# Five steps of the feed-forward generator, instead of four, per step of the output projection

## The chip, the cores and the metric

The kernel runs on the 8 cores of one Trainium2 chip. Each core computes 2 of 16 batch rows and exchanges nothing with the others. The metric is the device time of the slowest core in microseconds (us).

## The reference

Per batch row x is [2048, 1024]. The kernel computes `x + attention(xn) + ffn(xn)` with `xn` the layer norm of x. The feed-forward part is a loop of three rounds that carries `out`:

```python
out = x                                   # here x is xn
for _ in range(3):
    h = gelu(out @ w1 + b1); h = gelu(h @ w2 + b2); h = gelu(h @ w3 + b3)
    tf = sigmoid(h @ w4 + b4)             # one number per token
    combined = 0.7 * gf + 0.3 * tf        # gf: one number per batch row
    coupling = 0.1 + adaptive_range * (combined - 0.5) * 2.0
    out = out + coupling * twist(out)     # twist: quarters of the columns swapped, two negated
```

The widths are 1024, 1024, 512, 256, 1. The attention part ends with `out @ wo.T`, the output projection.

## The kernel before, in words

`build_program` lets Python generators record operations, and `Prog.emit` appends each to the list of its engine. Every engine runs its own list in the order of recording. `Prog.finalize` adds semaphore waits for true dependencies. All instructions are issued from `Prog.replay`, so the profile gives line 170 for all of them; they are told apart by tile names.

For each of the two batch rows (`for s in range(BATCH)`) come the layer norm (`gen_ln`), eight head pairs of attention (`gen_attention` beside `gen_projembed`), the normalisation (`gen_norm` beside `gen_gc`), and then four quarters of 512 tokens (`for q in range(NQ)`). A quarter has four token tiles of 128 rows, tq = 0 to 3. Only the quarters change. In them stand:

- `gen_ffn(q)`, 58 steps (a step ends at a `yield`). Steps 1 to 4: load an x tile into `xt0` or `xt1` by a DMA on SP, and write the normalised tile into `stream` (DVE). Then three rounds of 18 steps each. Steps 5 to 12, 23 to 30, 41 to 48: w1, a column block each (8 matmuls of 128x512 and a Gelu on ACT); in rounds 2 and 3 the first of them also casts and transposes the four stream tiles (`sbf`, `ofm`). Steps 13 to 16, 31 to 34, 49 to 52: w2. Steps 17 and 18, 35 and 36, 53 and 54: w3. Step 19 (37, 55): w4, tanh, `cpt`, four tiny matmuls, `cptm` and `ncptm`, and the update of stream tile 0 on DVE; the three steps behind it (20 to 22, 38 to 40, 56 to 58): the updates of tiles 1 to 3. An update is one copy into `t01` and four scalar_tensor_tensor.
- `gen_wo(q)`, 12 steps, three per token tile: (a) load the x tile into `xt0` (even tile) or `xt1` (odd tile), and 8 matmuls of `attn_in` by `woTt` into the first half of `ps_s0` or `ps_s1`; (b) 8 matmuls into the second half; (c) `tensor_add` of `ps_s` into the `xt` tile on DVE, and a DMA on SP that stores it into the DRAM scratch `ffn_s`, with the key `partD0` for even tiles and `partD1` for odd ones. The text calls these steps wo 1 to wo 12.
- `gen_final(q)`, recorded when both are done, four times: load a tile from `ffn_s` back into `xt0` or `xt1`, add it to `stream` (DVE), store the sum to `out`.

`drive((gen_ffn(q), 4), (gen_wo(q), 1))` sets the order: four steps of the first, one of the second, and so on until both end. With the rate 4, wo step n is recorded behind ffn step 4n, so wo 12 behind step 48.

The load of `gen_final` names both `partD0` and `partD1` as read:

```python
dma("sync", xb_t[:], ffn_s[s, tb * 128:(tb + 1) * 128, :],
    reads=["partD0", "partD1"], writes=[xb])
```

Of the kernel before, what the change touches and what calls it, by code (L numbers as in the profile page):

```python
# [185 lines left out]
def build_program(S=2048, BATCH=2, DM=1024, NH=16, dbg=False):  # L186
# [196 lines left out]
    def dma(queue, dst, src, reads, writes, note="", no_waw=False, **kw):  # L383
        return E(queue, "dma_start", dst, src, reads=reads, writes=writes, dma=True,
                 no_waw=no_waw, note=note, **kw)
# [116 lines left out]
    def drive(*pairs):  # L502
        gens = [g for g, n in pairs]
        rates = [n for g, n in pairs]
        done = [False] * len(gens)
        while not all(done):
            for gi in range(len(gens)):
                for _ in range(rates[gi]):
                    if not done[gi]:
                        done[gi] = next(gens[gi], _SENT) is _SENT  # L510
    _SENT = object()

    for s in range(BATCH):
# [352 lines left out]
        def gen_wo(q):  # L866
            for tq in range(QTB):
                tb = q * QTB + tq
                pp = tb % 2
                xb = f"xt{tb % 2}"  # L870
                xb_t = xt[tb % 2]
                dma("sync", xb_t[:], x_d[s, tb * 128:(tb + 1) * 128, :], reads=["dx"], writes=[xb])
                for half in range(DM // 512):
                    for c in range(CK):
                        E("tensor", "matmul", ps_s[pp][:, half * 512:(half + 1) * 512],
                          attn_in[c][:, tb * 128:(tb + 1) * 128],
                          woTt[c][:, half * 512:(half + 1) * 512],
                          start=(c == 0), stop=(c == CK - 1),
                          reads=[f"attnin{c}", f"woTtp{c}"], writes=[KS[pp]])
                    yield  # L880
                E("vector", "tensor_add", xb_t[:], ps_s[pp][:, 0:DM], xb_t[:],
                  reads=[KS[pp], xb], writes=[xb])
                dma("sync", ffn_s[s, tb * 128:(tb + 1) * 128, :], xb_t[:],
                    reads=[xb], writes=[f"partD{tb % 2}"], no_waw=True)
                yield
# [125 lines left out]
        def gen_final(q):  # L1011
            for tq in range(QTB):
                tb = q * QTB + tq
                xb = f"xt{tq % 2}"
                xb_t = xt[tq % 2]
                dma("sync", xb_t[:], ffn_s[s, tb * 128:(tb + 1) * 128, :],
                    reads=["partD0", "partD1"], writes=[xb])
                E("vector", "tensor_add", T["stream"][:, tq * DM:(tq + 1) * DM],
                  T["stream"][:, tq * DM:(tq + 1) * DM], xb_t[:],
                  reads=[f"stream{tq}", xb], writes=[f"stream{tq}"])  # L1020
                dma("sync", out_d[s, tb * 128:(tb + 1) * 128, :],
                    T["stream"][:, tq * DM:(tq + 1) * DM],
                    reads=[f"stream{tq}"], writes=[f"outD{tq}"], no_waw=True)
                yield

        for q in range(NQ):
            drive((gen_ffn(q), 4), (gen_wo(q), 1))
            for _ in gen_final(q):
                pass

# [12 lines left out]
def _get_nc(S, BATCH):  # L1043
    key = (S, BATCH)
    if key not in _NC_CACHE:
        _NC_CACHE[key] = build_program(S=S, BATCH=BATCH)
    return _NC_CACHE[key]
# [34 lines left out]
```

How the kernel before makes its waits and increments, by code:

```python
            def _run(engine):  # L164
                for op in self.ops[eng_name]:
                    for (sem, val) in op.waits:
                        engine.wait_ge(sem, val)
                    if op.method is None:
                        continue
                    inst = getattr(engine, op.method)(*op.args, **op.kwargs)
                    if op.inc_pos is not None:
                        kind, tgt = op.inc_pos
                        if kind == "D":
                            inst.then_inc(self.dma_slots[tgt], 16)
                        else:
                            inst.then_inc(self.eng_sems[tgt], 1)
```

## Time and profile before

| | us |
|---|---|
| two runs | 4245.42 and 4086.72, median 4166.07 |
| profiled execution | 4085.43 |
| its span, slowest core (2) | 4083.9 |
| spans of the 8 cores | 4058.0 to 4083.9 |
| PE busy | 2626.8 (64%) |
| DVE busy | 1402.4 (34%) |
| ACT busy | 1642.5 (40%) |

The profile is of core 2. Times in rows are microseconds from the start of the span, and a row of the timeline merges instructions of one kind that follow each other. PE is TensorE, DVE is VectorE, ACT is ScalarE, SPq is the queue of SyncE, which only issues DMAs here. The quarters of the first batch row lie between about 1437 and 2107 us, those of the second between about 3391 and 4084 us.

### The profile page before, as it was taken

The page shows a single profiled execution, that of the slowest core. Times are in us where ns is not written, and L with a number is a line of the kernel's source. Part 1 is how long each engine was busy: PE and PEld are TensorE (multiplying, and loading weights), DVE is VectorE, ACT ScalarE, POOL GpSimd, SP SyncE. Part 2 cuts the span into 40 slices and gives each one's busy share as a digit, 9 for nine tenths or more (in the row PEclk, how much of TensorE's full clock was granted, in tenths as well). Part 3 has the DMA queues.
Part 4 walks back from the last instruction along what each step waited for, and adds up shares of the span by engine and source line. Part 5 has one row for each costly group of instructions (what it writes and reads, how often), then busy time and mean ns, then how long its engine had stood idle before and what let it go on. Part 6 is the DMA issues. An engine that isn't in the chain of part 4 may idle for free.

```text
span 4083.9 us, 35532 instructions; the slowest of 8 cores (4058.0 to 4083.9 us)
## 1 busy us (share of the span) xinstructions
PE 2626.8 (64%) x10297; PEld 1084.6 (27%) x10486; DVE 1402.4 (34%) x2359; ACT 1642.5 (40%) x2082; POOL 40.5 (1%) x80
## 2 busy tenths in 40 slices
PE   0437777677767967567523576777767787666664
PEld 0213222232222223223212222232223212322322
DVE  5353233322332323333346333323332242333333
ACT  2206565566655022122123465666656701222221
POOL 1000000000000000000000000000000000000000
PEclk9959898898888578778666788998889857877776
DMA  6540011100100131121233011001110003022121
GB/s 158 129 82 22 13 27 26 25 8 21 26 19 5 27 91 67 48 92 42 72 110 110 23 26 26 16 11 26 26 25 15 7 13 78 31 93 73 42 83 57
DMA packets 84371, 193.23 MB, mean 47 GB/s; under 512 B 25559, under 2 KB 28632, under 8 KB 84184
## 3 DMA queue, kind: packets, MB, share of 16 engines
q1 hardware_dynamic: 73240, 175.74, 14.4%
q0 software_dynamic: 10944, 15.21, 2.8%
q8 instruction: 91, 1.49, 0.2%
q14 instruction: 96, 0.79, 0.1%
HBM read 134.27 MB, written 41.94 MB: 43 GB/s over the span
## 4 chain that ended last, share of the span: by engine, by line
PE 46%; DVE 22%; DMA 13%; issue 12%; ACT 5%; SPq 1%; DVEq 1%; POOL 0%; ACTq 0%; POOLq 0%
PE ps_w L170 24%; PE ps_s L170 14%; PE ps_pv L170 8%; DVE stream L170 6%; DMA xt<-x 4%; ACT pt L170 3%; DMA tmp<-qmag 3%; DMA xt<-ffn_s 3%; DVE vp L170 2%; DVE qh L170 2%; DVE ke L170 1%; DMA ke<-kmag 1%; SPq L170 1%; DMA w1t<-cnw 1%; DVE tmp L170 1%
## 5 line engine op out<-in xcount | busy, mean ns | idle before, releaser
L170 ACT ACTIVATE pt<-ps_s,cpool 128x1024 bf16<-128x1024 f32 x1024 | 1084.4, 1112 | 818.3 <-PE ps_s L170 814.9
L170 PE MATMUL ps_pv<-pt,vp 128*65 128x512 bf16 x2048 | 662.8, 407 | 291.9 <-DVE tmpB L170 229.6
L170 PE MATMUL ps_s<-qh,ke 128*128 128x512 bf16 x1976 | 645.7, 408 | 114.1 <-ACT pt L170 82.0
L170 PEld LDWEIGHTS ps_pv<-pt,vp 128*65 128x65 bf16 x2048 | 236.5, 118 | 573.6 <-issue 383.8
L170 PEld LDWEIGHTS ps_s<-qh,ke 128*128 128x128 bf16 x2048 | 173.6, 103 | 471.8 <-issue 394.5
L170 ACT ACTIVATE h<-ps_w,b1f 128x512 bf16<-128x512 f32 x192 | 131.9, 687 | 354.0 <-PE ps_w L170 354.0
L170 PE MATMUL ps_w<-ofm,w1t 128*128 128x512 bf16 x994 | 244.9, 405 | 15.5 <-DVE ofm L170 10.4
L170 ACT CAST ofm<-ps_w 128x128 bf16<-128x128 f32 x256 | 49.6, 280 | 457.3 <-PE ps_w L170 457.2
L170 PE MATMUL ps_w<-ident,sbf 128*128 128x128 bf16 x512 | 64.7, 306 | 248.0 <-DVE sbf L170 248.0
L170 DVE COPY rowstg<-ps_pv 1x1024 f32<-1x1024 f32 x32 | 39.1, 1222 | 455.7 <-PE ps_pv L170 455.4
L170 PE MATMUL ps_w<-xnfm,wvt 128*128 128x512 bf16 x498 | 170.2, 476 | 13.1 <-DVE ke L170 8.4
L170 DVE CAST vp<-ps_w 128x64 bf16<-128x64 f32 x512 | 115.6, 226 | 182.0 <-PE ps_w L170 154.3
L170 PE MATMUL ps_w<-ident,tmpv 128*128 128x128 bf16 x256 | 57.1, 223 | 178.2 <-DVE vp L170 170.7
L170 PE MATMUL ps_w<-h,w2t 128*128 128x512 bf16 x750 | 170.0, 379 | 0.9
L170 DVE CAST tmpv<-ps_w 128x512 bf16<-128x512 f32 x64 | 44.2, 691 | 335.3 <-PE ps_w L170 335.3
L170 PE MATMUL ps_s<-woTtp,attnin 128*128 128x512 bf16 x502 | 147.7, 444 | 7.9 <-DMA woTtp<-woT_s 5.1
L170 PE MATMUL ps_w<-xnfm,wqt 128*128 128x512 bf16 x494 | 135.5, 399 | 24.7 <-DMA wqt<-wqT_s 21.4
L170 DVE COPY xsq<-ps_pv 1x1024 f32<-1x1024 f32 x32 | 39.1, 1222 | 322.4 <-PE ps_pv L170 322.4
L170 PE MATMUL ps_w<-ident,xnb 128*128 128x128 bf16 x256 | 33.0, 306 | 175.9 <-DVE xnb L170 169.9
L170 PEld LDWEIGHTS ps_w<-ofm,w1t 128*128 128x128 bf16 x1024 | 104.7, 103 | 149.4 <-issue 46.0
L170 PE MATMUL ps_s<-rcps,onesf 1*64 1x512 f32 x128 | 116.8, 1063 | 36.3 <-DMA rcps<-rowsums 36.3
L170 PE MATMUL ps_w<-xnfm,wkt 128*128 128x512 bf16 x499 | 130.0, 384 | 6.1 <-DVE ke L170 2.8
(128 smaller groups left out, 2608.9 us busy)
## 6 DMA issues: line engine op xcount, KB each, us to landing
xt<-x SPq DMA_DIRECT2D x128, 512.0 KB, 4.0
ffn_s<-xt SPq DMA_DIRECT2D x32, 512.0 KB, 2.6
xt<-ffn_s SPq DMA_DIRECT2D x32, 512.0 KB, 4.1
out<-stream SPq DMA_DIRECT2D x32, 512.0 KB, 3.0
ke<-kmag SPq DMA_DIRECT2D x32, 256.0 KB, 4.0
qh<-qmag SPq DMA_DIRECT2D x32, 256.0 KB, 4.0
tmp<-qmag SPq DMA_DIRECT2D x32, 256.0 KB, 3.8
wqt<-wqT_s SPq DMA_DIRECT2D x16, 256.0 KB, 3.0
```

Source lines behind the costliest of these rows:

```text
L170: inst = getattr(engine, op.method)(*op.args, **op.kwargs)
```

## The change

One number: the rate of the feed-forward generator.

```diff
         for q in range(NQ):
-            drive((gen_ffn(q), 4), (gen_wo(q), 1))
+            drive((gen_ffn(q), 5), (gen_wo(q), 1))
             for _ in gen_final(q):
                 pass
```

wo step n is now recorded behind ffn step 5n, as long as there are any: wo 11 behind step 55, and wo 12 behind step 58, the last. No operation is added or removed, and the list of SP is the same in both kernels, waits included.

DVE, end of the first quarter, before. `sbf` and `ofm` are the cast and transposed stream of round 3, `xt<-ps_s,xt` is the add of a wo step (c), `stream<-stream,xt` the add of `gen_final`, `cpt` and `cptm` the coupling.

```order
477 L170 CAST ofm_78<-ps_w 128x128
478 L170 TENSOR_TENSOR xt<-ps_s,xt 128x1024
479 L170 TENSOR_SCALAR cpt<-cpt,smallt 1x512
...
500 L170 SCALAR_TENSOR_TENSOR stream<-t_95,ncptm,stream 128x256
501 L170 SCALAR_TENSOR_TENSOR stream<-t_95,cptm,stream 128x256
502 L170 TENSOR_TENSOR stream<-stream,xt 128x1024 x4
503 L170 TENSOR_SCALAR stream<-xt,rstat,mr 128x1024 x4
504 L170 TENSOR_TENSOR xt<-ps_s,xt 128x1024
```

The row 478 is wo 12 and stands ahead of the updates of round 3; behind the last update comes `gen_final` at once.

The same place on DVE after.

```order
477 L170 CAST ofm_78<-ps_w 128x128
478 L170 TENSOR_TENSOR xt<-ps_s,xt 128x1024
479 L170 TENSOR_SCALAR cpt<-cpt,smallt 1x512
...
500 L170 SCALAR_TENSOR_TENSOR stream<-t_95,ncptm,stream 128x256
501 L170 SCALAR_TENSOR_TENSOR stream<-t_95,cptm,stream 128x256
502 L170 TENSOR_TENSOR xt<-ps_s,xt 128x1024
503 L170 TENSOR_TENSOR stream<-stream,xt 128x1024 x4
504 L170 TENSOR_SCALAR stream<-xt,rstat,mr 128x1024 x4
505 L170 TENSOR_TENSOR xt<-ps_s,xt 128x1024
```

The row 478 is now wo 9, and wo 12 has moved to row 502, behind the last update and ahead of the four adds of `gen_final`.

PE, from the coupling at the end of the first quarter to the coupling of round 1 in the second, before. `ps_s<-woTtp,attnin` are wo matmuls, `w4t` and `onesf,cpt` belong to the coupling; between the rows shown are w1, w2 and w3 matmuls only.

```order
1670 L170 MATMUL ps_w<-h_1_94,w4t 1x512
1671 L170 MATMUL ps_w<-onesf,cpt 128x1 x4
1672 L170 MATMUL ps_s<-woTtp,attnin 128x512 x8
...
1704 L170 MATMUL ps_s<-woTtp,attnin 128x512 x8
...
1769 L170 MATMUL ps_s<-woTtp,attnin 128x512 x8
...
1779 L170 MATMUL ps_w<-h_1_94,w4t 1x512
1780 L170 MATMUL ps_w<-onesf,cpt 128x1 x4
1781 L170 MATMUL ps_s<-woTtp,attnin 128x512 x8
```

The same place on PE after.

```order
1669 L170 MATMUL ps_w<-h_1_94,w4t 1x512
1670 L170 MATMUL ps_w<-onesf,cpt 128x1 x4
1671 L170 MATMUL ps_s<-woTtp,attnin 128x512 x8
...
1679 L170 MATMUL ps_s<-woTtp,attnin 128x512 x8
...
1720 L170 MATMUL ps_s<-woTtp,attnin 128x512 x8
...
1778 L170 MATMUL ps_w<-h_1_94,w4t 1x512
1779 L170 MATMUL ps_w<-onesf,cpt 128x1 x4
1780 L170 MATMUL ps_s<-woTtp,attnin 128x512 x8
```

Three groups of wo matmuls stand between the two couplings in both, and one behind the second; they have moved by one group, since the first of the three is now wo 11 of the quarter before.

## Rows read from the trace of the kernel before

**Rows 1.** Chain that ended last, by line, whole span.

```profile
PE ps_w L170 24%; PE ps_s L170 14%; PE ps_pv L170 8%; DVE stream L170 6%; DMA xt<-x 4%; ACT pt L170 3%; DMA tmp<-qmag 3%; DMA xt<-ffn_s 3%; DVE vp L170 2%; DVE qh L170 2%; DVE ke L170 1%; DMA ke<-kmag 1%; SPq L170 1%; DMA w1t<-cnw 1%; DVE tmp L170 1%
```

**Rows 2.** That chain, second quarter's end: start us, us, what.

```profile
1764.64 0.06 DVE stream L170
1764.70 0.34 issue
1765.04 1.23 DVE stream L170
...
1766.34 0.34 SPq L170
...
1766.73 4.88 DMA xt<-ffn_s
...
1773.43 4.29 DMA xt<-ffn_s
...
1786.14 5.36 DMA xt<-x
...
1792.63 3.55 DMA xt<-x
...
1797.31 3.45 DMA xt<-x
...
1802.00 0.54 DVE cpt L170
```

**Rows 3.** Timeline of PE, 1735 to 1830 us: start, busy, instructions, idle before.

```profile
1783.37 0.38 PE L170 MATMUL ps_w<-h,w4t 128*1 128x512 bf16 x1 [0.49 <-ACT h L170]
1802.67 1.83 PE L170 MATMUL ps_w<-onesf,cpt 1*128 1x1 f32 x8 [18.92 <-DVE cpt L170]
1823.38 1.01 PE L170 MATMUL ps_w<-ident,sbf 128*128 128x128 bf16 x8 [1.91 <-DVE sbf L170]
```

**Rows 4.** Timeline of DVE, 1725 to 1830 us.

```profile
1733.28 1.23 DVE L170 TENSOR_TENSOR xt<-ps_s,xt 128x1024 f32<-128x1024 f32 x1 [9.54 <-PE ps_s L170]
1764.64 0.48 DVE L170 SCALAR_TENSOR_TENSOR stream<-t,cptm,stream 128x256 f32<-128x256 f32 x1
1765.04 1.22 DVE L170 TENSOR_TENSOR stream<-stream,xt 128x1024 f32<-128x1024 f32 x1
1771.70 1.22 DVE L170 TENSOR_TENSOR stream<-stream,xt 128x1024 f32<-128x1024 f32 x1 [5.45 <-DMA xt<-ffn_s]
```

**Rows 5.** Timeline of SP's queue: second quarter, and the last quarter (4031.69, 4034.51).

```profile
1734.63 0.33 SPq L170 DMA_DIRECT2D ffn_s<-xt  x1
1737.29 0.33 SPq L170 DMA_DIRECT2D xt<-ffn_s  x1
1766.34 0.34 SPq L170 DMA_DIRECT2D out<-stream  x1
1766.73 0.43 SPq L170 DMA_DIRECT2D xt<-ffn_s  x1
...
4031.69 0.33 SPq L170 DMA_DIRECT2D ffn_s<-xt  x1
4034.51 0.33 SPq L170 DMA_DIRECT2D xt<-ffn_s  x1
```

**Rows 6.** DMA issues, whole span: count, size, median us to landing; then one tile's range.

```profile
ffn_s<-xt SPq DMA_DIRECT2D x32, 512.0 KB, 2.6
xt<-ffn_s SPq DMA_DIRECT2D x32, 512.0 KB, 4.1
DMA to landing us min/median/max: 2.6/3.1/5.8
```

**Rows 7.** PE, start of the first quarter, and a wo group of the second.

```profile
1455.06 7.54 PE L170 MATMUL ps_w<-xnfm,w1t 128*128 128x512 bf16 x25 [1.46 <-DMA w1t<-cnw]
1763.23 1.89 PE L170 MATMUL ps_s<-woTtp,attnin 128*128 128x512 bf16 x8
```

**Rows 8.** The chain in round 2's w1: start us, us, matmuls.

```profile
1827.95 3.89 PE ps_w L170 x10
1831.89 8.15 PE ps_w L170 x37
```

**Rows 9.** Stretches: us, busy of PE, PEld, DVE, ACT, POOL, PEclk, DMA share, GB/s.

```profile
1783.00:1802.00 19.00, 0.38 (x1) 0.08 (x1) 5.62 (x7) 0.91 (x2) 0.00 (x0) 0.60 0.52 175
1817.00:1828.00 11.00, 4.09 (x33) 3.17 (x34) 5.31 (x19) 3.09 (x16) 0.00 (x0) 0.50 0.00 0
1832.00:1850.00 18.00, 17.95 (x83) 8.10 (x83) 0.00 (x0) 6.38 (x10) 0.00 (x0) 1.00 0.09 30
```

## The prediction

> **What bounds the kernel now.** I read the chain that ended last, first by line and then in order of time, because the change touches only eight places (four quarters for each of two batch rows). By line, loads of `xt` from x and from `ffn_s` hold 4% and 3% of the span, and DVE's `stream` 6% [rows 1]. In order of time these loads all stand at the joint between two quarters [rows 2]. The last stream update ends, `gen_final` adds its first tile at 1765.04, and then come three reloads from `ffn_s`, three x loads and the coupling of the next quarter at 1802.00. Each reload has an issue, the flight and an add of 1.22 us around it, one behind the other, because SP's queue puts the store of a result ahead of the next reload. PE is no part of that stretch: its matmuls of round 1 end with the w4 matmul at 1783.37, and it then sits idle for 18.92 us until DVE has made `cpt` [rows 3]. So a joint is bound by the loop of DVE, SP and DMA, and anything that starts its first link later moves the whole rest, with no PE work to take up the slack.
>
> The one link that is free now is the first reload. The add of wo 12 starts at 1733.28 [rows 4], its store is issued at 1734.63 and the first reload at 1737.29 [rows 5], some 28 us ahead of the add that wants it at 1765.04. That add waits for nothing [rows 4].
>
> **The change part by part.**
>
> *DVE, wo 12.* Its add now stands behind the last stream update, in the slot that starts at 1765.04. It waits for the matmuls of wo 11, which are recorded behind step 55 and so run during some 12 us of stream updates, and for an x load whose queue place has not changed; both are done. Cost: everything from here is late by the add and what follows it. From the start of the add to the issue of its store is 1734.63 - 1733.28 = 1.35 us [rows 4, 5].
>
> *SP, store and first reload.* The queue is the same list in both kernels, so the first reload still stands behind this store, and it still waits until both `partD` stores have landed. That wait is shown: in the second quarter the reload is issued 1737.29 - 1734.63 = 2.66 us behind the store, in the last one 4034.51 - 4031.69 = 2.82 [rows 5]; over the eight quarters the mean is 2.68. The median landing of such a store is 2.6 us [rows 6]. I take 2.68.
>
> *The first reload's flight.* It is no longer hidden. The three later reloads take 4.29 to 4.88 us in the chain, but each runs beside the 512 KB store of a result that was issued 0.4 us ahead of it [rows 2, 5]. The first has nothing beside it. The nearest rows of a lone 512 KB load are the x loads at 1792.63 and 1797.31 with 3.55 and 3.45 us [rows 2]; the median of all reloads, the hidden ones too, is 4.1 [rows 6]. I take 3.7 and 0.05 for the start of the add. Bounds: 3.45 below, and 5.8 above, the longest landing of any transfer with `ffn_s` [rows 6].
>
> The sum per quarter is 1.35 + 2.68 + 3.75 = 7.8 us. Below it stands 1.35 + 2.64 + 3.45 = 7.4 (2.64 is the shortest of the eight gaps), above it 1.35 + 2.82 + 5.8 = 10.0.
>
> The Trainium skill (DMA: Bandwidth & Descriptors, the section on where the fixed 2 us of a DMA goes) speaks against the change more strongly than these rows: a semaphore fires only when the target memory has confirmed the last byte, and this is slowest for a write to HBM. By that rule the store into `ffn_s` should cost at least what the reload costs, 4.1 us, and the sum would be 1.35 + 4.1 + 4.1 = 9.5 per quarter, 76 in all. The trace does not agree here: the store lands in 2.6 us and the reload in 4.1 [rows 6], so the measurement decides.
>
> *How often.* Eight quarters. In seven the joint leads to more work that starts late: in six the next quarter, whose coupling of round 1 waits for DVE behind the x loads, and once the layer norm of the second batch row, whose first loads stand behind the same reloads on SP. The eighth is the end of the kernel. Nothing hides any of them: PE's 18.92 us of idle in the joint only grow [rows 3]. Eight times 7.8 is 62 us.
>
> *PE, groups of wo matmuls.* A group of 8 takes 1.89 us [rows 7]. Count them where PE sets the time. Round 2 has two groups with either rate (wo 7 and 8 before, wo 5 and 7 after), round 3 one (wo 11 before, wo 10 after). The gaps in which DVE updates the stream have one each in rounds 1 and 2, in the shadow of some 12 us of DVE work; wo 11 is new in the gap of round 3, again in that shadow. Round 1 loses wo 4, but in the six quarters that follow another one its end waits for DVE anyway, as just shown, so this returns nothing there. In the first quarter of a batch row PE is what is waited for: it starts in earnest when the last w1 tile lands at 1455.06 [rows 7]. Before, from there to the coupling, run the last matmul of the first block, seven blocks of w1, four of w2, two half-sized of w3 and the groups wo 2 and wo 4, since wo 1 went ahead during the wait for w1. After, wo 1 stands behind the first block and wo 4 behind the coupling. One group comes onto the path and one leaves it: 0, with the clock at most 2 us either way, twice.
>
> *DVE, wo 3, 6 and 9.* Each moves by at most one slot and stays beside PE work: wo 6 keeps its place behind the transposes of round 2, wo 9 takes that of wo 12 in round 3, wo 3 stays ahead of the coupling. Cost 0. If a cover went, each would cost 1.22 us, 8 x 1.22 = 10 for one of them.
>
> *The sum.* The profiled execution took 4085.43 us, 1.5 more than its span of 4083.9. With 62 it is 4148, 1.5% more. The median of the two runs shown, 4166.07, stands 80.6 above the profiled execution, because one of them took 4245.42; the other, 4086.72, agrees with the profiled one. I forecast on that level. If the time of the changed kernel is a median over two such values, it stands near 4148 + 81 = 4229, and I let the range reach there.
>
> **The rivals.**
>
> *Only the queue is waited for.* If the first reload did not need the landing of the last store, only its place behind it on SP, the joint would grow by 1.35 + 0.4 (an issue) + 3.75 = 5.5 us, in all 44, and the time 4129. Against it stands the gap of 2.66 to 2.82 us between the issues in every quarter, where nothing else holds SP [rows 5].
>
> *The change is hidden.* Time 4085. It would need another engine to be last in the joint. Against it: PE idles for 18.92 us there and DVE waits 5.45 us for a reload [rows 3, 4].
>
> *The clock gives it back (the other side: not slower).* The granted clock is 0.50 (1.2 GHz) in the transposes behind the round 1 gap and 1.00 (2.4 GHz) in w1 behind them [rows 9]. The first 10 matmuls take 3.89 us, the next 37 take 8.15 [rows 8], so the 10 cost 3.89 - 10 x 0.22 = 1.7 us more than at the full clock. The four batches of transposes take 1.01 us each [rows 3], some 0.5 more than at twice the clock, 2.0 in all. If moving wo groups kept PE at the full clock through the gaps of rounds 1 and 2, that would return 2 x 3.7 = 7.4 us a quarter, 59 in all, and the time would be 4089, no change. It decides from where the clock is full at the first transpose. Against it: both gaps keep one group of the same size at the same place, and about 10 us of PE idle stay behind it.
>
> The Trainium skill (TensorE: Matmul & The Clock Gate, the part on what is observed) says that the throttled clock is the default and that activity releases it. The rows agree, 0.50 behind the gap and 1.00 in w1; the rule gives the changed kernel no more activity in these gaps than before.
>
> *More than the sum.* If the reload lands as slowly as the slowest, 10.0 us a quarter make 80, and one DVE add that loses its cover 10 more: 4176, which is over 2%. It decides at 10.2 us a quarter. For it: the traffic of eight cores in one stage, 175 GB/s on this core in the joint [rows 9]. Against it: the first reload flies alone.
>
> **How the numbers follow.** The forecast (7.4 to 10 us a quarter, 4144 to 4165) has 0.75, the queue alone 0.06, hidden 0.03, the clock 0.04, more than the sum 0.12. Within 2%, which is about what a measurement of this kernel can tell from no change, fall the first four; 2% of 4086.7 is 82 us. I leave 0.01 for faster and move 0.02 to slower for what I have not seen: faster 0.01, same 0.85, slower 0.14. The predicted time is 4148. The range starts at the case of the queue alone, 4128, and ends at 4232 for the reason given with the sum; the mechanism's own range is 4140 to 4168.
>
> **What would show it.** In the profile of the changed kernel the add `xt<-ps_s,xt` should stand directly behind the last stream update of every quarter, its store be issued some 1.35 us later, the first reload 2.7 us after that, and the first `gen_final` add should have an idle time of about 6.5 us released by DMA `xt<-ffn_s`: 32 waits on that reload instead of 24. DVE's idle time ahead of these adds should grow by about 8 x 6.5 = 52 us, PE's wait for `cpt` in round 1 of a quarter from 18.9 to about 26.7 us. Rounds 2 and 3 should have the length that they have now. I am wrong if the gap between store and reload is under 1 us, if the granted clock of the transposes is above 0.50, or if the distance from one coupling of round 1 to the next grows by under 6 or over 10 us.

## The result and the profile after

| | before | after |
|---|---|---|
| median of all runs, us | 4095.73 (10 runs) | 4156.85 (11 runs) |
| lowest, us | 4084.39 | 4151.49 |
| profiled span, us | 4083.9 | 4151.9 |
| ratio | | 1.0166, interval 1.0135 to 1.0196 |

The change makes the kernel slower by 1.66%, about 68 us (1.35 to 1.96% are 55 to 80 us). The profiled spans differ by the same 68.0 us. Some executions ran with a lower granted clock on one die or both and took longer; the ratios leave them out, and one of the two times of before that were known at the prediction, 4245.42, was such a run.

The place that the prediction speaks of, the joint between the second and the third quarter, on DVE in the changed kernel (timeline of the slowest core, here core 7; start, busy time, instruction, idle time before it and its releaser; the first row is the copy that opens the last update):

```profile
1780.65 0.43 DVE L170 COPY t<-stream 128x512 f32<-128x512 f32 x1
...
1783.35 1.22 DVE L170 TENSOR_TENSOR xt<-ps_s,xt 128x1024 f32<-128x1024 f32 x1
1790.78 1.23 DVE L170 TENSOR_TENSOR stream<-stream,xt 128x1024 f32<-128x1024 f32 x1 [6.21 <-DMA xt<-ffn_s]
1797.03 1.23 DVE L170 TENSOR_TENSOR stream<-stream,xt 128x1024 f32<-128x1024 f32 x1 [5.03 <-DMA xt<-ffn_s]
...
1825.22 1.23 DVE L170 TENSOR_TENSOR xt<-ps_s,xt 128x1024 f32<-128x1024 f32 x1 [2.02 <-DMA xt<-x]
1826.36 0.53 DVE L170 TENSOR_SCALAR cpt<-cpt,smallt 1x512 f32<-1x512 f32 x1
```

The add of wo 12 stands where the first add of `gen_final` stood [rows 4], and the first add of `gen_final`, which waited for nothing, now waits 6.21 us for its reload. SP's queue over the same stretch:

```profile
1784.70 0.33 SPq L170 DMA_DIRECT2D ffn_s<-xt  x1
1787.38 0.33 SPq L170 DMA_DIRECT2D xt<-ffn_s  x1
1792.08 0.34 SPq L170 DMA_DIRECT2D out<-stream  x1
```

Store and reload are still 2.68 us apart, as before [rows 5], but they now stand behind the stream updates and no longer some 28 us ahead of the add that wants them. The chain that ended last shows the three links that were hidden, add, store and reload, one behind the other:

```profile
1783.35 1.23 DVE xt L170
...
1784.70 2.62 DMA ffn_s<-xt
...
1787.38 3.30 DMA xt<-ffn_s
...
1790.78 1.24 DVE stream L170
```

In this joint the sum of the prediction reads 1.35 + 2.68 + 3.40 = 7.43 us. Over the eight quarters on this core the distance from the add of wo 12 to the first add of `gen_final` is 7.3 to 10.1 us, 8.5 in the mean. In six of the eight the gap from store to reload is 2.67 to 2.72 us, in the other two 3.17 and 4.94, and from the issue of the reload to the add it takes 3.3 to 5.1, 4.1 in the mean. Over all eight cores, 64 ends of quarters, the distance from add to add is 7.9 us in the mean and 7.4 in the median. The groups of DVE, before and then after (busy, mean ns, idle before and its releaser):

```profile
L170 DVE TENSOR_TENSOR stream<-stream,xt 128x1024 f32<-128x1024 f32 x32 | 39.1, 1223 | 119.0 <-DMA xt<-ffn_s 119.0
```

```profile
L170 DVE TENSOR_TENSOR stream<-stream,xt 128x1024 f32<-128x1024 f32 x32 | 39.2, 1225 | 176.0 <-DMA xt<-ffn_s 176.0
```

57 us of waiting for reloads are new, over 32 waits in place of 24; the eight first adds, which waited for nothing before, wait 58.2 us in all. PE pays nothing in this stretch but waits longer for the coupling of round 1:

```profile
1802.45 0.38 PE L170 MATMUL ps_w<-h,w4t 128*1 128x512 bf16 x1 [0.49 <-ACT h L170]
1827.04 1.83 PE L170 MATMUL ps_w<-onesf,cpt 1*128 1x1 f32 x8 [24.21 <-DVE cpt L170]
1841.96 1.01 PE L170 MATMUL ps_w<-ident,sbf 128*128 128x128 bf16 x8 [9.57 <-DVE sbf L170]
```

PE was idle for 18.92 us there [rows 3], now for 24.21. In the mean over the six joints between quarters and all cores it was 18.6 us and is now 25.2. In the transposes the granted clock is 0.50 in both traces.

The table below cuts the whole execution at the 24 instructions `cptm<-ps_w` of DVE, one per round. Each number is the median over the eight cores of the distance between two of them, in us; where several quarters are named it is the mean of their medians.

| stretch | before | after | times |
|---|---|---|---|
| start to the first coupling | 1482.4 | 1487.5 | 1 |
| coupling of round 1 to round 2 | 55.9 | 56.2 | 8 |
| round 2 to round 3 | 53.3 | 53.5 | 8 |
| round 3 to round 1 of the next quarter (the joint) | 50.8 | 58.1 | 6 |
| the same across the two batch rows, with norm and attention | 1377.6 | 1385.7 | 1 |
| round 3 of the last quarter to the last add | 29.4 | 36.9 | 1 |

The joints hold 6 x 7.3 + 8.1 + 7.5 = 59.5 us of the 68. They grow by a little less than the 7.9 from add to add, since the loads behind it take 0.5 us less together. Rounds 2 and 3 keep their lengths within 0.3 us.

### The profile page after: what moved, and what is told of

Read it like the earlier page. It is cut to its first block, busy times and chain, and to the rows that moved or that the text cites. A ratio compares the mean times of both kernels' runs of the same rounds, so it can differ in the third digit from the quotient of the medians.

```text
span 4151.9 us, 35721 instructions; the slowest of 8 cores (4126.2 to 4151.9 us)
## 1 busy us (share of the span) xinstructions
PE 2659.1 (64%) x10486; PEld 1084.4 (26%) x10486; DVE 1402.6 (34%) x2359; ACT 1645.2 (40%) x2082; POOL 40.5 (1%) x80
## 4 chain that ended last, share of the span: by engine, by line
PE 45%; DVE 22%; DMA 14%; issue 11%; ACT 5%; SPq 1%; DVEq 1%; POOL 0%; ACTq 0%; POOLq 0%
PE ps_w L170 23%; PE ps_s L170 14%; PE ps_pv L170 8%; DVE stream L170 6%; DMA xt<-x 4%; DMA xt<-ffn_s 3%; ACT pt L170 3%; DMA tmp<-qmag 3%; DVE vp L170 2%; DVE qh L170 2%; DVE ke L170 1%; DMA ke<-kmag 1%; SPq L170 1%; DMA w1t<-cnw 1%; DVE tmp L170 1%
## 5 line engine op out<-in xcount | busy, mean ns | idle before, releaser
L170 PE MATMUL ps_s<-qh,ke 128*128 128x512 bf16 x2048 | 663.7, 408 | 103.1 <-ACT pt L170 79.6
L170 PE MATMUL ps_w<-ident,tmpv 128*128 128x128 bf16 x256 | 57.2, 223 | 178.4 <-DVE vp L170 170.9
L170 PE MATMUL ps_s<-woTtp,attnin 128*128 128x512 bf16 x512 | 158.0, 465 | 0.0
L170 PE MATMUL ps_w<-onesf,cpt 1*128 1x1 f32 x192 | 33.3, 290 | 186.2 <-DVE cpt L170 186.2
L170 DVE TENSOR_SCALAR cpt<-cpt,smallt 1x512 f32<-1x512 f32 x24 | 12.7, 531 | 405.5 <-ACT cpt L170 405.5
```

The source lines that it names most:

```text
L170: inst = getattr(engine, op.method)(*op.args, **op.kwargs)
```

## The experiments

All ratios are to the kernel before, timed on the same chip. The profile quoted is of the slowest core of each kernel.

**Only wo 12 held back (rate 4).** If the loss is the place of one add and its store, this alone must cost what the change costs.

```diff
-            drive((gen_ffn(q), 4), (gen_wo(q), 1))
+            gw = gen_wo(q)
+            drive((gen_ffn(q), 4), ((next(gw) for _ in range(11)), 1))
+            for _ in gw:
+                pass
```

> Rate 4 as before, but wo 12 alone (its add on DVE and its store on SP) is recorded behind the last stream update. Theory A (the store and the first reload are laid bare at each of eight joints): all of the loss is there, 8 x 7.5 = 60 us, ratio to the kernel before 1.014 to 1.016, about as the changed kernel. Rival B (the moved groups of matmuls cost, not the store): ratio 1.000 to 1.004, since every matmul keeps its place.

Measured: 1.0226, interval 1.0155 to 1.0297. This excludes rival B, but the interval is too wide to say that it is the same loss, so it was run again beside the changed kernel.

> The kernel of e1 again, beside the changed kernel on the same chip. Theory A (the place of wo 12 is the whole loss): the same time as the changed kernel, ratio 1.014 to 1.018. Rival B (the other groups give something back or cost something): more than 0.4% apart from it.

> The changed kernel itself, as the reference for the run with only wo 12 held back: ratio 1.015 to 1.018 by either theory.

Measured: 1.0165 (1.0130 to 1.0200) with only wo 12 held back, and 1.0150 (1.0135 to 1.0165) for the changed kernel. In the cut by couplings the six joints have 56.6 to 58.0 us (mean 57.6) against 57.2 to 60.0 (58.4), and from the last coupling to the last add it takes 36.7 against 36.6. So moving one add and one store behind the last update is the whole loss as far as these runs can tell, and what the eleven other steps moved by the rate cost or give is below the intervals, which are 0.35% and 0.15% to either side.

**Each reload waits for the stores of its own parity only (rate 5).**

```diff
                 dma("sync", xb_t[:], ffn_s[s, tb * 128:(tb + 1) * 128, :],
-                    reads=["partD0", "partD1"], writes=[xb])
+                    reads=[f"partD{tb % 2}"], writes=[xb])
```

> Rate 5, but each reload of gen_final waits only for the stores of its own parity, so the first one is issued right behind the store of wo 12 without waiting for its landing. Theory A: the first add of gen_final comes at 1.35 + 0.4 + about 4.4 = 6.2 us behind the last update in place of 7.5 to 7.8, 11 to 13 us less in all: ratio about 1.013 to 1.014. Rival C (the wait for the landing is nothing, the place in the queue is all): no difference from the changed kernel, 1.0166.

Measured: 1.0113 (1.0063 to 1.0163). In SP's queue and on DVE, second quarter:

```profile
1779.06 0.33 SPq L170 DMA_DIRECT2D ffn_s<-xt  x1
1779.48 0.62 SPq L170 DMA_DIRECT2D xt<-ffn_s  x1
```

```profile
1777.71 1.22 DVE L170 TENSOR_TENSOR xt<-ps_s,xt 128x1024 f32<-128x1024 f32 x1
1784.30 1.23 DVE L170 TENSOR_TENSOR stream<-stream,xt 128x1024 f32<-128x1024 f32 x1 [5.37 <-DMA xt<-ffn_s]
```

The reload is issued 0.42 us behind the store in place of 2.68, but it then flies beside the store and takes 4.8 us in place of 3.4 in this joint. Over the 64 ends of quarters of all cores it takes 4.5 us to the add in place of 3.4 (means), and from add to add it is 6.3 us where the changed kernel has 7.9. The joints between quarters are shorter by 1.1 us (57.0). The timed ratio cannot tell 1.0113 from 1.0150; the trace does. The wait for the landing is a part of the price, and the place in the queue is another.

The same edit does something else, outside the joint. Earlier in the second quarter of this run:

```profile
1737.68 0.33 SPq L170 DMA_DIRECT2D ffn_s<-xt  x1
1738.16 0.33 SPq L170 DMA_DIRECT2D xt<-x  x1
```

The x load behind a store of `gen_wo` is issued 0.48 us after it. In the changed kernel the same load comes 2.68 us after the store (1742.89 and 1745.57 in its trace), though it fills the other `xt` buffer, so that wait was no true dependency of the data. It comes from the bookkeeping in `Prog.emit`: a store counts every earlier reload with its key as something it depends on, and a later load into a buffer waits for all operations that depended on that buffer's DMAs (`slot_cons`). With both keys in `reads`, each store is tied to the reloads of both buffers. This matters for rate 3 below.

**The first reload ahead of the store of wo 12 (rate 5).** The tile that it reads was stored long ago.

```diff
+                if tq == QTB - 1:          # gen_wo, ahead of the add of wo 12
+                    t0 = q * QTB
+                    dma("sync", xt[0][:], ffn_s[s, t0 * 128:(t0 + 1) * 128, :],
+                        reads=["partD0"], writes=["xt0"])
                 E("vector", "tensor_add", xb_t[:], ps_s[pp][:, 0:DM], xb_t[:],
...
-                dma("sync", xb_t[:], ffn_s[s, tb * 128:(tb + 1) * 128, :],
-                    reads=["partD0", "partD1"], writes=[xb])
+                if tq > 0:                 # gen_final
+                    dma("sync", xb_t[:], ffn_s[s, tb * 128:(tb + 1) * 128, :],
+                        reads=[f"partD{tb % 2}"], writes=[xb])
```

> Rate 5, but the first reload is recorded on SP ahead of the store of wo 12 (it reads a tile stored long ago). wo 11 and wo 12 stay at the end. Theory A: the first add of gen_final waits for nothing again; left are the add of wo 12 (1.2 us) and a second reload that waits for the landing of the store, together some 2.4 us a joint, 19 us in all: ratio 1.004 to 1.006. Rival B: still 1.015 to 1.017.

Measured: 1.0054 (1.0027 to 1.0081). DVE:

```profile
1776.58 1.22 DVE L170 TENSOR_TENSOR xt<-ps_s,xt 128x1024 f32<-128x1024 f32 x1
1777.71 1.22 DVE L170 TENSOR_TENSOR stream<-stream,xt 128x1024 f32<-128x1024 f32 x1
1784.16 1.23 DVE L170 TENSOR_TENSOR stream<-stream,xt 128x1024 f32<-128x1024 f32 x1 [5.23 <-DMA xt<-ffn_s]
```

Two thirds of the loss are gone with one DMA moved, while wo 11 and wo 12 are still last. What is left is the add, 1.13 us, and a second reload whose buffer waits for the landing of that store: from the first add to the second it is 7.1 us, against 6.3 before (means over all cores). Together these are 2.0 us a joint, where 2.4 were expected, and the joints between quarters are 2.1 us longer than before.

**wo 11 and wo 12 pulled ahead (rate 5 until wo 10).**

```diff
-            drive((gen_ffn(q), 4), (gen_wo(q), 1))
+            gf, gw = gen_ffn(q), gen_wo(q)
+            for _ in range(10):
+                for _ in range(5):
+                    next(gf)
+                next(gw)
+            for _ in gw:
+                pass
+            for _ in gf:
+                pass
```

> Rate 5 until wo 10, and then wo 11 and wo 12 directly behind it, at step 50, ahead of the coupling of round 3. Theory A: the joint is as short as before; round 3 has two groups of matmuls (wo 10 and wo 11) where before had one, 8 x 1.7 = 14 us at most: ratio 1.001 to 1.004. Rival B (a higher rate costs by itself): ratio 1.015.

Measured: 1.0078 (1.0033 to 1.0123), whose lower part overlaps what was expected. The joint is 50.6 us again, and the stretch from round 2 to round 3 has 55.2 in place of 53.3: 1.9 us for one group of matmuls more on PE's path, as expected. Eight of these are 15 us, 0.4%. The lowest times of the two kernels, 4093.84 and 4079.62 us, are 14 us apart, which fits; the rest of the ratio is not placed.

**Other rates.** With rate 3 wo 12 goes further ahead, with rate 6 three wo steps stand at the end.

```diff
-            drive((gen_ffn(q), 4), (gen_wo(q), 1))
+            drive((gen_ffn(q), 3), (gen_wo(q), 1))
```

> Rate 3: wo 12 behind step 36. Theory A (a cliff: what counts is whether the last store is behind the last update): no gain from moving it further ahead; PE has three groups in round 2 and none in round 3, none in the gap of round 2, and one group more on PE's path in the first quarter of a batch row, 2 x 1.9 us: ratio 0.999 to 1.003. Rival D (a slope: each step of the rate costs the same): ratio about 0.984.

> Rate 6: wo 10, 11 and 12 behind step 58, wo 8 behind step 48 in round 3. Theory A (a cliff): the joint is as long as with rate 5, and PE has two groups in round 3 where it had one, 8 x 1.7 = 14 us: ratio 1.017 to 1.022. Rival D (a slope): twice the loss of rate 5, ratio 1.03 or more.

Measured: rate 6 has 1.0196 (1.0171 to 1.0220), as theory A has it. Rate 3 has 1.0202 (1.0130 to 1.0275), and both its expectations are wrong: rate 3 costs about as much as rates 5 and 6. Its joint is 60.5 us long, 9.7 more than before. DVE in one of them:

```profile
1819.64 1.22 DVE L170 TENSOR_TENSOR xt<-ps_s,xt 128x1024 f32<-128x1024 f32 x1
1828.01 1.22 DVE L170 TENSOR_TENSOR xt<-ps_s,xt 128x1024 f32<-128x1024 f32 x1 [7.15 <-DMA xt<-x]
1829.15 0.53 DVE L170 TENSOR_SCALAR cpt<-cpt,smallt 1x512 f32<-1x512 f32 x1
```

```profile
1820.93 0.33 SPq L170 DMA_DIRECT2D ffn_s<-xt  x1
1823.70 0.33 SPq L170 DMA_DIRECT2D xt<-x  x1
```

Before, one add of a wo step (wo 3) stands ahead of the coupling of round 1. With rate 3 there are two, since wo 6 is recorded behind step 18, one step ahead of the coupling. The x load of wo 6's tile (recorded by wo 4) stands on SP behind the store of wo 3 and is issued 2.77 us after it, and DVE, which runs in order, waits for it with the coupling behind. It is the same round trip, add, store, load, 8.37 us from add to add, in another place. PE is not the reason: its last w4 matmul starts at 1804.38, and it then waits 25.06 us for the coupling. The wait between this store and this load is the needless one that the run with own parities removed; rate 3 with that edit was not tried. The theory of the second round trip was tested by itself.

```diff
-            drive((gen_ffn(q), 3), (gen_wo(q), 1))
+            gf, gw = gen_ffn(q), gen_wo(q)
+            for fs in range(1, 59):
+                next(gf)
+                n = {18: 0, 21: 0, 23: 2}.get(fs, 1 if fs % 3 == 0 else 0)
+                for _ in range(n):
+                    next(gw, None)
...
```

> Rate 3, but wo 6 and wo 7 are recorded behind step 23 in place of 18 and 21. Theory F (rate 3 lost because the add of wo 6 stood ahead of the coupling of round 1 and waited for an x load that waited for the store of wo 3, a second round trip of 8.4 us in the joint): the joint is 50 to 51 us again; round 2 has four groups of matmuls where the kernel before has two and round 3 none where it has one, 8 x 1.7 = 14 us, and 4 us more at the two first quarters: ratio 1.003 to 1.006. Rival G (a low rate costs by where the matmuls are): 1.015 or more, joint 58 to 60 us.

Measured: 1.0066 (1.0047 to 1.0086), the joint 53.2 us. The round trip is gone. The joint is 2.4 us longer than in the kernel before, which was not expected: with rate 3, wo 1 is recorded behind step 3, so its x load stands on SP ahead of the x load of stream tile 3. With rate 3 it takes 11.9 us from the first stream tile to the add of wo 3 (1807.71 to 1819.64), in the changed kernel 9.9 (1815.32 to 1825.22). In this run it is 11.7 us from the first stream tile to the last, against 7.0 before, and 1.9 from there to the coupling, against 4.2 (means over all cores). The matmul groups cost what was expected: from the coupling of round 1 to that of round 3 a quarter is 1.8 us longer.

**A shorter joint (rate 4).** The runs so far fit a joint that is a serial loop on SP and DVE. Then other orders must shorten it. First, both first reloads at the start of `gen_final`, and the next reload ahead of the store of a result:

```diff
         def gen_final(q):
+            ld(0)                      # ld(tq): the reload of tile tq into xt[tq % 2]
+            ld(1)
             for tq in range(QTB):
...
-                dma("sync", xb_t[:], ffn_s[s, tb * 128:(tb + 1) * 128, :],
-                    reads=["partD0", "partD1"], writes=[xb])
                 E("vector", "tensor_add", T["stream"][:, tq * DM:(tq + 1) * DM],
...
+                if tq + 2 < QTB:
+                    ld(tq + 2)
                 dma("sync", out_d[s, tb * 128:(tb + 1) * 128, :],
```

> Rate 4, gen_final with both first reloads recorded at its start and each further reload ahead of the store of a result. Nothing left out. Theory A (the joint is a serial loop of add, issue and reload): the second add waits for nothing and the third and fourth reload overlap, some 10 us less a joint: about 4005 us, ratio 0.98. Rival E (the joint is bound by the bytes that the DMAs move): under 3 us a joint, ratio above 0.994.

Measured: 0.9822 (0.9805 to 0.9839), 4011.44 us. The joint is 41.4 us long, 9.4 less than before.

Second, two more tiles `fb0` and `fb1` of 4 KB per partition, in the 8 KB that the layout reserves for `gw1t`, which is never loaded:

```diff
-        cur = place(f"gw1t_{k}", [128, DM // 2], BF16, cur)
+    cur = place("fb0", [128, DM], F32, cur)
+    cur = place("fb1", [128, DM], F32, cur)
...
+        FB = [(T["fb0"], "fb0"), (T["fb1"], "fb1"), (xt[0], "xt0"), (xt[1], "xt1")]
...
+            for tq in range(QTB):      # gen_final: four reloads, then four adds and stores
+                tb = q * QTB + tq
+                dma("sync", FB[tq][0][:], ffn_s[s, tb * 128:(tb + 1) * 128, :],
+                    reads=["partD0", "partD1"], writes=[FB[tq][1]])
```

The x loads of steps 1 to 4 use the same four tiles.

> Rate 4, with two more buffers of 4 KB in space reserved for weights that are never loaded there: all four reloads are issued ahead of the first add, and the next quarter's four x loads have a buffer each. Nothing left out. Theory A: the joint shrinks by 12 to 17 us, where PE's round 1 becomes the bound (it ends at 1783.4 where the coupling was at 1802.0): 3950 to 3990 us, ratio 0.967 to 0.977. Rival E (bytes): no better than f1.

Measured: 0.9707 (0.9688 to 0.9726), 3965.39 us, faster than both kernels. DVE in a joint:

```profile
1754.65 2.35 DVE L170 TENSOR_TENSOR stream<-stream,fb 128x1024 f32<-128x1024 f32 x2
1756.92 2.35 DVE L170 TENSOR_TENSOR stream<-stream,xt 128x1024 f32<-128x1024 f32 x2
1766.65 0.81 DVE L170 TENSOR_SCALAR stream<-fb,rstat,mr 128x1024 f32<-128x1024 f32 x1 [7.37 <-DMA fb<-x]
```

and PE at its end:

```profile
1772.92 0.38 PE L170 MATMUL ps_w<-h,w4t 128*1 128x512 bf16 x1 [0.49 <-ACT h L170]
1775.58 1.20 PE L170 MATMUL ps_w<-onesf,cpt 1*128 1x1 f32 x8 [2.28 <-DVE cpt L170]
```

The four adds wait for nothing, and PE's idle time at the coupling has fallen from 18.92 [rows 3] to 2.28 us, and to 2.3 in the mean over all cores and joints between quarters, where it has 1.6 in the other rounds. The joint is 33.8 us long and practically PE's: of the 34 us from 1740 to 1774, PE is busy for 31.1.

Last, the change itself on top of that kernel: does PE, now nearly the bound, hide the store?

```diff
-            drive((gen_ffn(q), 4), (gen_wo(q), 1))
+            drive((gen_ffn(q), 5), (gen_wo(q), 1))
```

> The kernel with four buffers, with rate 5. Theory A (the round trip stands in the joint whatever the rest of it looks like): the first add of gen_final again comes 7.5 us or more later, and since four reloads now fly at once perhaps 10 us; PE hides only the 2.3 us by which the coupling waits for DVE less nothing: 7 to 11 us a joint, 56 to 88 us more than with rate 4, ratio 0.984 to 0.992. Rival H (with four buffers PE bounds the joint and hides the store): within 0.3% of 0.9707.

Measured: 0.9916 (0.9902 to 0.9931), just inside what theory A gives and far from rival H. The rate costs 0.9916 - 0.9707 = 2.1% of the kernel before here, with about 0.25% to either side, where the change cost 1.66%. The joint grows from 33.8 to 45.6 us, by 11.8:

```profile
1613.41 1.22 DVE L170 TENSOR_TENSOR xt<-ps_s,xt 128x1024 f32<-128x1024 f32 x1
1622.96 2.50 DVE L170 TENSOR_TENSOR stream<-stream,fb 128x1024 f32<-128x1024 f32 x2 [8.33 <-DMA fb<-ffn_s]
...
1636.84 0.81 DVE L170 TENSOR_SCALAR stream<-fb,rstat,mr 128x1024 f32<-128x1024 f32 x1 [8.90 <-DMA fb<-x]
```

From add to add it is 9.55 us in this joint and 8.2 in the mean over all cores, 0.4 more than with two buffers, since a reload with three others behind it takes 3.8 us in place of 3.4. The four `gen_final` adds, which followed each other within 3.4 us at rate 4, now take 5.3 from the first to the last, as they wait for later reloads too, and the wait for the first x tile is 8.90 here in place of 7.37. A better tail does not protect against a producer that is recorded last: all four reloads were hidden by the updates, and all four are laid bare.

## Why the prediction was right and wrong

*The mechanism.* Right. The joint of DVE, SP and DMA sets the end, PE is no part of it, and the first reload was the free link. The runs that hold back wo 12 alone (the whole loss) and that issue the first reload ahead of the store (two thirds of it gone) show this directly.

*The sum of one joint.* 7.8 us were forecast. The median over the cores is 7.3 for the six joints between quarters, 8.1 across the batch rows and 7.5 at the end. The terms themselves add up to 7.9 from add to add, in the mean of the 64 ends of quarters, and that this is so near 7.8 is in part luck, since two terms were off in opposite ways. Store to reload was put at 2.68 and is 3.07 in the mean (2.68 in the median): 24 of the 64 gaps are over 2.8 us, up to 4.96, where only 1 of 64 was before. Flight and start of the add were put at 3.75 and are 3.45 in the mean. The prediction took the flight from the x loads at 1792.63 and 1797.31 as lone loads, but each had another x load in flight (issued at 1793.87, landed at 1798.07). The hidden first reloads of that same trace, which do fly alone, land after 3.12 to 3.48 us. The add to store is 1.35, as forecast. One joint of 10.1 us on the slowest core lies just above the upper bound of 10.0, and not for the reason given there: its store held the reload for 4.94 us, and the reload took 3.77 to the add.

*How often.* Right, eight times, 59.5 us of joints against the 62 of the sum. From one coupling of round 1 to the next it is 7.8 us more, between the 6 and 10 beyond which the prediction called itself wrong.

*PE's groups.* Right at 0. Rounds 2 and 3 keep their lengths within 0.3 us, and in the first quarter of a batch row it takes 30.6 us from the last w1 tile to the coupling before (1455.06 to 1485.66, core 2), and 30.5 after on the same core (1460.87 to 1491.36), although wo 1 stands behind that landing and wo 4 no longer ahead of the coupling.

*The signs that were named.* The idle time of the first add was put at 6.5 us; it is 7.3 in the mean of the slowest core's eight and 6.7 over all cores. DVE's idle time ahead of these adds was to grow by about 52 us and grew by 57.0. PE's wait for the coupling was put at 26.7 us and is 25.2 in the mean; in the joint shown it is 24.21, where the distance from the last update to the coupling grew by only 6.1 us (1765.04 to 1802.00 before, 1783.35 to 1826.36 after) and PE ended its round 1 0.8 us later. The transposes kept their 1.01 us and their granted clock of 0.50, so the clock gave nothing back. Queue alone (4129) and hidden (4085) are excluded by the ratio and by the gap of 2.68 us, no change by the clock (4089) by the ratio too. More than the sum (4176) needed 10.2 us a quarter, and only single joints come near that. The rule of the Trainium skill (DMA: Bandwidth & Descriptors, where the fixed 2 us goes), by which a store to HBM would cost no less than the reload and the sum be 76 us, is not borne out here: 2.62 us for the store, 3.30 for the reload in the chain above, and 3.0 against 3.4 in the mean of 64.

*What failed: the level.* The step that failed is "The median of the two runs shown, 4166.07, stands 80.6 above the profiled execution", and what I made of it. The sum says slower by 62 us. But the predicted time, 4148, stands below the 4166.07 that was shown for the kernel before, so as a forecast against that number it reads as a small gain, and the kernel became slower by 1.66% with an interval that excludes no change. The working and the final number say opposite things about the direction. Ten runs of the kernel before have their median at 4095.73; the 4166.07 was the mean of two runs that lie 159 us apart. I noticed the gap, kept the number at the level of the profiled execution, and put the doubt into the upper end of the range, 4232, where none was needed: the median after is 4156.85, inside the mechanism's own range of 4140 to 4168. The remaining 68 - 59.5 = 8.5 us are not in the sum. 5.1 of them lie ahead of the first coupling, where both kernels run the same instructions until shortly before; in the second profile of the changed kernel that distance is about 1 us above before, and with rate 4 it is 1483.8 and 1485.7 in the two kernels with another `gen_final` against 1482.4, so most of it is scatter between executions. The second measurement of the changed kernel, 1.0150, is 61 us. The 0.85 on within 2% came true, and the ratio is within 2%, but that weight should have been called slower in direction.

*What was not seen at all.* That the rate before sits between two cliffs, at 3 and at 5. The prediction looked only up. The same reading of the order, one step down, would have shown a second wo add ahead of the coupling.

## What to carry to other kernels

When two generators are interleaved, what matters of a rate is not where most of the work lands but whether a producer of something that is stored and loaded back falls behind the last independent work of its consumer: here one add and one store cost 7.5 us, eight times, and one DMA moved ahead of them gave two thirds back. Read the lists of the in-order engines at the serial joints, in both directions of a tuning number, before trying its neighbours. And when a serial loop of load, add and store bounds a joint, issue the next load ahead of the store and look for dead space for more buffers: that was worth 2.9% here, more than any rate that was tried. Last, a semaphore wait that the data does not need can hide in the bookkeeping until another order puts it on the path: compare each wait in the trace with the buffers of the two operations.

## What the runs showed of the hardware

A 512 KB reload issued 0.42 us behind a 512 KB store of the same core landed 4.0 us after its issue, against 3.2 when it was issued after the landing of the store, and the store itself took 2.9 us in place of 2.6 (medians of 64 each, in the run with own parities and in the changed kernel). Being issued 2.65 us sooner behind the store gave 1.6 us in the mean from add to add, and 0.8 in the joint shown.

The store into the DRAM scratch landed sooner than a load of the same size, 2.6 us against 3.2, but not always. In the kernel before, 1 of 64 stores of wo 12 held the reload for over 2.8 us; in the changed kernel, where the store is issued behind the last update, 24 of 64 did. On the slowest core these were two of eight, 3.17 and 4.94 us, with nothing else of that core in flight. What delayed them was not tried.
